# Graph network kernel, attention stage: scores computed with features on partitions, weights of batches and units drawn together, and a new order of the work on each engine

## The reference

```python
x = _layernorm(x + _L0_gnn_ref(x, L0_gnn_W, src, dst))      # three hops, then x @ W.T
edge_feat = concatenate([x[src], x[tgt]], axis=1)           # 256 values per edge
h = relu(edge_feat @ W1 + b1)                               # 128 values
w = sigmoid(h @ W2 + b2)[:, 0]                              # one weight per edge
agg = segment_sum(w[:, None] * x[src], tgt, num_segments=3125)
out = _layernorm(_layernorm(x + agg) * gamma + beta)        # outer norm of the residual sum left out here
```

## Time and profile before

| | before |
|---|---|
| median of 3 runs | 1422.31 us (1417.19 to 1425.18) |
| profiled execution: its own time | 1416.73 us |
| its span, first to last instruction | 1415.0 us |
| mean granted clock of TensorE | 0.831 |
| busy: PE, DVE, ACT, POOL | 1016.7 (72%), 980.4 (69%), 672.6 (48%), 655.3 (46%) us |
| gathers (L891) | 464, from 573.5 to 1346.3 us |
| moved by the gathers' queue | 60.85 MB |

### The profile page before, as it was taken

How to read it: one execution, slowest core, us unless ns; L and a number is a source line. 1 busy time by engine, 2 the same in 40 slices (tenths; PEclk the granted TensorE clock), 3 DMA queues, 4 the chain that set the end, 5 groups by cost and what they waited for, 6 DMA issues and landing times.

```text
span 1415.0 us, 32758 instructions
## 1 busy us (share of the span) xinstructions
PE 1016.7 (72%) x9885; PEld 784.0 (55%) x9886; DVE 980.4 (69%) x3477; ACT 672.6 (48%) x2508; POOL 655.3 (46%) x789
## 2 busy tenths in 40 slices
PE   4766665998998999236776777667686776777870
PEld 3656565777787877124554555445455554555550
DVE  7988887899998886136566656555565665566677
ACT  6555555211000222026655666556565656566676
POOL 1000001366743676755555565545556565555602
PEclk9999999999999999558678768667768787877785
DMA  2000000000000111535454455445445554544511
GB/s 82 1 0 0 0 0 1 1 3 3 2 3 4 38 41 52 142 116 144 133 148 140 141 150 147 122 121 144 140 135 157 143 145 127 153 138 144 153 34 47
DMA packets 77263, 120.07 MB, mean 85 GB/s; under 512 B 20488, under 2 KB 39484, under 8 KB 77116
## 3 DMA queue, kind: packets, MB, share of 16 engines
q0 software_dynamic: 22272, 60.85, 15.5%
q1 hardware_dynamic: 54844, 57.44, 13.9%
HBM read 111.41 MB, written 6.81 MB: 84 GB/s over the span
## 4 chain that ended last, share of the span: by engine, by line
DVE 37%; PE 28%; another core or an unknown queue 14%; issue 12%; ACT 5%; POOL 2%; DVEq 1%; DMA 0%; ACTq 0%; POOLq 0%; SPq 0%
PE bank L1748 6%; DVE t L1346 5%; DVE stage L997 4%; DVE region L1412 4%; PE bank L1633 4%; PE bank L1835 3%; DVE region L1396 3%; DVE region L1428 2%; PE bank L1787 2%; ACT PQ L2104 2%; PE bank L1635 2%; PE bank L1848 2%; PE bank L1709 2%; DVE stage L1160 2%
## 5 line engine op out<-in xcount | busy, mean ns | idle before, releaser
L891 POOL DMA_INDIRECT region<-src_split,region x464 | 444.9, 959 | 328.2 <-PE bank L1802 113.0
L1346 DVE SCALAR_TENSOR_TENSOR t<-bank,vec 128x128 f32<-128x128 f32 x464 | 107.0, 286 | 198.0 <-remote 166.8
L1748 PE MATMUL bank<-U,region 128*128 128x256 f16 (+1 forms) x1875 | 235.2, 276 | 3.8 <-DVE U L1137 2.1
L1826 PE MATMUL bank<-xs,region 128*128 128x128 f16 x572 | 130.8, 250 | 131.5 <-DVE region L1412 81.8
L2104 ACT ACTIVATE PQ<-region 128x128 f32<-128x128 f32 x572 | 169.7, 300 | 65.4 <-issue 37.4
L1748 PEld LDWEIGHTS bank<-U,region 128*128 128x128 fp8e4 x1875 | 178.8, 98 | 35.7 <-DVE U L1137 2.8
L2093 ACT CAST region<-bank 128x512 f16<-128x512 f32 x286 | 152.7, 579 | 89.6 <-remote 53.3
L1988 ACT CAST region<-bank 128x500 f32 x202 | 119.7, 593 | 92.2 <-PE bank L1635 68.4
L1826 PEld LDWEIGHTS bank<-xs,region 128*128 128x128 f16 x572 | 64.3, 112 | 150.5 <-issue 150.2
L1828 PE MATMUL bank<-region 128*128 128x128 f16 x572 | 134.7, 256 | 13.0 <-issue 12.9
L1848 PE MATMUL bank<-region 128*128 128x256 f16 x572 | 124.4, 349 | 24.9 <-issue 20.7
(11 more groups left out here) (272 smaller groups left out, 2360.2 us busy)
## 6 DMA issues: line engine op xcount, KB each, us to landing
region<-slot_rows SPq DMA_DIRECT2D x143, 256.0 KB
region<-src_split,region POOLq DMA_INDIRECT x464
region<-in_dst_dram SPq DMA_DIRECT2D x116, 64.0 KB
region<-tgt_split SPq DMA_DIRECT2D x116, 16.0 KB
src_split<-U SPq DMA_DIRECT2D x25, 64.0 KB, 1.5
src_split<-xs SPq DMA_DIRECT2D x25, 64.0 KB, 1.5
tgt_split<-q SPq DMA_DIRECT2D x25, 64.0 KB, 1.6
slot_rows<-aggT SPq DMA_DIRECT2D x88, 3.2 KB
```

Of the source, the lines that this page charges most:

```text
L891: nc.gpsimd.indirect_dma_start(out=G[:, p * TPS + i, :], out_offset=None, in_=src_split, in_offset=bass.IndirectOffsetOnAxis(ap=listed[n % ...
L1346: z = nc.vector.scalar_tensor_tensor(out=spare[i][:, :], in0=bank[q % 2][:, i * P:(i + 1) * P], scalar=0.0, in1=vec[:, W2, :], op0=ALU.max ...
L1748: z = nc.tensor.matmul(bank[2 * (k % 2) + p][:, 0:width], count[:, h, b * P:(b + 1) * P], U[k % 2][:, h, 0:width], start=h == 0, stop=h == ...
L1826: nc.tensor.matmul(to, here, p_table[:, h, 0:D], start=True, stop=False)
```

## The change

The score is no longer summed by DVE and ACT, but by PE. Before the hops, DVE takes the sign of W2 into a column `signs` and multiplies W1 and b1 by |W2|, so that the score becomes the sum over features of relu(...) * sign. In the loop:

1. PE computes P + Q with *features* on partitions and edges along the row (the operands of the products change places; L1810 and L1815 for a batch, L1875 and L1878 for a unit).
2. ACT takes relu of the whole 128x512 bank into float16 (`batch_relu`, `pair_relu`), and DVE the difference between the float32 relu and it (`batch_rest`, `pair_rest`), one instruction each.
3. PE sums both over the partitions by products with `signs`, one output column per tile: 8 products for a batch, 8 for a unit (`add_features`, for step s - 1), into bank 6.
4. One pair of sigmoids on ACT and one split on DVE serve batch and unit of a step together.
5. Order: `fetch_pair` stands ahead of `scored` in PE's step and `sums` at its end; `sums` and `sum_pair` follow their batch or unit by three steps and not by two. ACT and DVE take the unit first, DVE begins with `add_sums` and ends with the split and the weighing. SP loads a unit's slots one step earlier.
6. Buffers: `turned_hot`, `hot_weights` and `ohW` get three, `y_rows` four. `STEPS` is 149, and the batches are spread over the first 146.

The core of the diff (left out: buffers, semaphores, the checks of input ranges, the new places of folding):

```diff
+            link(nc.vector.tensor_tensor(yT[:, :], vec[:, W2, :], x3T[:, :], ALU.mult))
+            nc.vector.tensor_tensor(w1s[:, :, :], w1s[:, :, :],
+                                    yT[:, :].unsqueeze(1).broadcast_to([P, 2, D]), ALU.mult)
...
-                for i in range(m):
-                    z = nc.vector.scalar_tensor_tensor(
-                        out=spare[i][:, :], in0=bank[q % 2][:, i * P:(i + 1) * P], scalar=0.0, in1=vec[:, W2, :],
-                        op0=ALU.max, op1=ALU.mult, accum_out=zs[q % 2][:, i:i + 1])
+            def batch_rest(b):
+                dve.wait_ge(batch_high, b + 1)
+                nc.vector.scalar_tensor_tensor(
+                    out=relu_low[BATCH][b % 2][:, :], in0=bank[b % 2][:, :], scalar=0.0, in1=relu_high[BATCH][b % 2][:, :],
+                    op0=ALU.max, op1=ALU.subtract).then_inc(batch_low, 1)
...
+            def pair_rest(u):
+                dve.wait_ge(pair_high, u + 1)
...
-                    for half in range(2):
-                        z = nc.tensor.matmul(bank[q % 2][:, i * P:(i + 1) * P],
-                                             ohT[p][q * QR:(q + 1) * QR, i * P:(i + 1) * P],
-                                             qwin[p][q * QR:(q + 1) * QR, half * D:(half + 1) * D],
+                        z = nc.tensor.matmul(bank[q % 2][:, i * P:(i + 1) * P],
+                                             G[:, first + i, half * D:(half + 1) * D], ident16[:, :],
                                              start=False, stop=i == m - 1 and half == 1)
                 z.then_inc(s_psum, 1)
...
+            def add_features(s):
+                b, u = batch_at[s], unit_at(s)
...
+                if b is not None:
+                    pe.wait_ge(batch_low, b + 1)
+                if u is not None:
+                    pe.wait_ge(pair_low, u + 1)
+                if scored_steps(s) > 1:
+                    pe.wait_ge(w_ready, scored_steps(s) - 1)
...
+                    for i in range(TPB):
+                        to = bank[6][:, kind * TPB + i:kind * TPB + i + 1]
+                        nc.tensor.matmul(to, relu_high[kind][k % 2][:, i * P:(i + 1) * P], signs[:, :],
+                                         start=True, stop=False)
+                        z = nc.tensor.matmul(to, relu_low[kind][k % 2][:, i * P:(i + 1) * P], signs[:, :],
+                                             start=False, stop=True)
+                z.then_inc(z_psum, 1)
...
                 if u:
-                    pe.wait_ge(pair_z_ready, u)
+                    pe.wait_ge(pair_low, u)
...
+                if 0 <= u < TOTAL:
+                    fetch_pair(u)
                 if b is not None:
                     scored(b // BPS, b // BPS % 2, b % BPS)
-                    if b >= 2:
-                        sums((b - 2) // BPS, (b - 2) // BPS % 2, (b - 2) % BPS)
-                if 0 <= u < TOTAL:
-                    fetch_pair(u)
-                if 0 <= u - 2 < TOTAL:
-                    sum_pair(u - 2)
+                if s:
+                    add_features(s - 1)
+                if 0 <= u - 3 < TOTAL:
+                    if u == 3:
+                        pe.wait_ge(flag_ready, 1)
+                    sum_pair(u - 3)
...
+                if b is not None and b >= 3:
+                    sums((b - 3) // BPS, (b - 3) // BPS % 2, (b - 3) % BPS, blocks_folded(s - 1))
...
+                if 0 <= u < TOTAL:
+                    pair_relu(u)
+                    copy_rows(u)
                 if b is not None:
-                    sigmoids(b // BPS, b // BPS % 2, b % BPS)
+                    batch_relu(b)
+                if s and (batch_at[s - 1] is not None or unit_at(s - 1) is not None):
+                    sigmoids(s - 1)
```

More of the change, by code:

```diff
@@ L69, in gnn_kernel, with unit_at, scored_steps, batches_until @@
     for b in range(BATCHES_POOLED):
-        batch_at[b * STEPS // BATCHES_POOLED] = b
+        batch_at[b * (STEPS - 3) // BATCHES_POOLED] = b
+    def unit_at(s):
+        return s - LEAD if 0 <= s - LEAD < TOTAL else None
+    def scored_steps(s):
+        return sum(batch_at[k] is not None or unit_at(k) is not None for k in range(s + 1))
+    def batches_until(s):
+        return sum(b is not None for b in batch_at[0:max(s + 1, 0)])
+    def units_until(s):
+        return min(max(s + 1 - LEAD, 0), TOTAL)
+    FOLD_STEP = UNITS + 4 + LEAD
+    def batches_summed(s):
+        return max(batches_until(s) - 3, 0) if s < STEPS else BATCHES_POOLED
+    def blocks_folded(s):
+        return sum(due(k, FOLD_STEP, UNITS, DENSE - 1) is not None for k in range(s + 1))
+    def columns_at(s):
+        return 0 if batch_at[s] is not None else TPB, TPB if unit_at(s) is None else 2 * TPB
     def due(at, first, every, end):
@@ L298, in gnn_kernel @@
         Qs = [PQ[i][:, D:2 * D] for i in range(2)]
+        relu_high[BATCH] = [PQ[i][:, :].bitcast(f16) for i in range(2)]
         q16 = [sb(f"q16{i}", [P, 2, D], f16) for i in range(2)]
@@ L301, in gnn_kernel @@
         tiles_before = sb("tiles_before", [P, 1], f32)
-        spare = t1 + t2
-        unused = [PQ[i // 2][:, i % 2 * D:(i % 2 + 1) * D] for i in range(4)]
         ident16 = sb("ident16", [P, P], f16)
@@ L306, in gnn_kernel @@
         ws = [sb(f"ws{i}", [P, TPB], f32) for i in range(2)]
-        wsplit = [sb(f"wsplit{i}", [P, TPB, 2], f16) for i in range(2)]
-        ohW = [sb(f"ohW{i}", [P, TPB, 2, JW], f16) for i in range(2)]
+        ohW = [sb(f"ohW{i}", [P, TPB // 2, 2, 2, JW], f16) for i in range(3)]
         fbn = [[sb(f"fbn{r}{i}", [P, GROUP, 6], f32) for i in range(2)] for r in range(2)]
@@ L1510, in _ @@
                 b = batch_at[s]
[L1511 to L1519 removed]
+                after = None if s == 0 or batch_at[s - 1] is None else batch_at[s - 1] + 1
+                if after is not None and after % BPS == 0:
+                    first = load_four(ET.DVE, base[4], after // BPS, N)
+                attend(s, b, after, None if first is None else first[(after or 0) % BPS])
+            last_firsts = [dve.value_load(base[4][0:1, b + 4:b + 5], min_val=0, max_val=N)
+                           for b in range(BATCHES_POOLED - 3, BATCHES_POOLED)]
+            for b, first_target in zip(range(BATCHES_POOLED - 3, BATCHES_POOLED), last_firsts):
                 add_sums(b, b % BPS, first_target)
@@ L1778, in scored @@
                     pe.wait_ge(ohT_ready, n + 1)
-                if not (is_static(b) and b < 2):
-                    pe.wait_ge(z_ready, b - 1)
+                if b >= 2:
+                    pe.wait_ge(batch_low, b - 1)
+                for half in range(2):
+                    nc.tensor.matmul(bank[q % 2][:, 0:m * P], qwin[p][q * QR:(q + 1) * QR, half * D:(half + 1) * D],
+                                     ohT[p][q * QR:(q + 1) * QR, 0:m * P], start=half == 0, stop=False)
                 pe.wait_ge(gathered[p * BPS + q], 32 * (n - p) + 16 * m)
-                for half in range(2):
-                    nc.tensor.matmul(bank[q % 2][:, 0:m * P].rearrange("p (t k) -> p t k", k=P), ident16[:, :],
-                                     G[:, first:first + m, half * D:(half + 1) * D], start=half == 0, stop=False)
                 for i in range(m):
@@ L1803, in sums @@
                                              G[:, tile, (2 + y_half) * D:(3 + y_half) * D],
-                                             ohW[q % 2][:, i, w_half, :], start=i == 0 and y_half + w_half == 0,
+                                             ohW[b % 3][:, i // 2, w_half, i % 2, :], start=i == 0 and y_half + w_half == 0,
                                              stop=i == m - 1 and y_half == 1)
```

286 lines of the change are left out of this document (143 added, 143 removed).

## The result

The changed kernel takes 1412.9 us (median of 17 runs, 1410.6 to 1415.7), the kernel before 1422.2 us (17 runs, 1417.1 to 1430.4): ratio 0.9943, 95% interval 0.9925 to 0.996. It is faster by 0.6%, where 3.6% slower was forecast. A second set gave 1414.1 against 1419.1 us, 0.996 (0.9939 to 0.9981). The two profiled executions, 1412.6 and 1415.0 us, are closer than the medians, so I read sizes from two profiles of each kernel.

The account below looks back on a forecast made before the run. The prediction took POOL's gather cycle, with PE's increments held, as the bound. Longer pauses (+48) and the start (+3) summed to +51 us, 1473 against the median 1422.3; range 1410 to 1530.

Parts of the forecast that it names:

- The bound: Gather stage: POOL's cycle bounds, as PE's semaphore increments are held until about 1.0 us after a batch's last gather.
- The step that failed: PE's step after a release: 18 of 46 products, `sums` included, exceed the run-ahead limit, lengthening POOL's pause by 0.9 us.
- the +48: POOL's pauses: half of 107 grow by 0.9 us because `sums` comes after the release, +48 us.
- The mean of the pauses: POOL's pause before a gather batch: 2.0 us on average, 0.57 above 1.43.
- DVE and ACT at 0: Both engines get lighter, but neither is the bound, so their relief was costed at 0.
- One-column products: PE's step: priced at the 0.026 us spacing of `sums` products, 0.42 us a step at full clock.
- Their 72 us: PE's added work over the stage from one-column products, taken as hidden in PE's 27% idle time if the order is right.
- The start: Before `sums` of batch 0: three more hand-overs, mostly within the long hold, then two links and half a PE step, +3 us.
- C: Rival, faster: deeper buffers and three-batch lag get `agg_psum` out before each release; pauses fall to 1.43 us: -61, 1361; chance 0.17.
- B: Rival: the run-ahead limit does not bind; only PE's longer step shows, in cycles at half clock: +18, 1440; chance 0.20.
- D: Rival, much slower: every pause grows by 1.4 us, from one-column weight loads or `add_features` needing its own release: +150, 1572; chance 0.15.

Follow-up runs that it names:

- columns_less: The changed kernel without the eight one-column products of the relu's lower parts: 1218.6 us, ratio 1.0051 to the kernel before, which takes 1212.7 there.

## Why the prediction was wrong

**The bound** was read rightly for the chip of the first runs: POOL's cycle, PE's increments held until about 1.0 us after the last gather; without gathers a step falls from 5.4 to 3.65 us.

**The step that failed** is "`agg_psum` is ready at R + 1.35 + 4.4 ... behind `pair_psum` ... stand 46 products, and 28 can be issued", and with it the +48. I let PE's step begin at the release with `fetch_pair`. It does not: at the release PE stands in the step before, with `scored` or the one-column products still to issue. These, `sum_pair` and `sums` need less of this release than `fetch_pair` does. In the cycle shown, with the release near 877.7, the one-column products need the sigmoid that ends at 878.23 and `sums` needs the `add_sums` that ends at 879.20, both there before PE comes to them; the relu and the difference for `fetch_pair` take until 879.80. So `sum_pair` starts at 879.06 and `sums` at 879.86, 4.1 us and more ahead of the release near 884.0 at which they come out, and both ahead of the 10 products of `fetch_pair`. The first increment held is that of the one-column products, with `sums` only 4 products behind it; what is left over for after the release is work that POOL does not wait for. `pair_psum` is held, as forecast, and `fetch_pair` waits for its relu and difference, as forecast, but `sums` no longer stands behind them. The mechanism itself exists: with 8 or 16 more products `sums` falls behind the release in 65 and 79 of 80 cycles. The cost of the 16 is near what it says, but not its pattern: `sums` is late in nearly all cycles, and the ordinary pauses grow by 0.34 us on average, where I had 0.9 in half of them.

**The mean of the pauses** was a mean over two kinds. "Half of 107 pauses grow by 0.9" had no such cause: the extra 0.57 us over 1.43 was the 25 long ones. I had the rows for it (148 steps, 116 batches) and did not sort them.

**DVE and ACT at 0** was wrong. In a long pause nothing hides the round: 0.69 us more of DVE cost 16.7 us in all, and the change took the long pauses from 3.57 to 2.86 us, 0.7 x 24 = 17 us. How much of that is the relief and how much the new order on the engines no run separates. I had written that it would matter "were PE's increments free", and in one cycle of four they are. The other pauses grew by 0.1, 7 us over the same batches.

**One-column products** at 0.026 us: 0.025 measured. The Trainium skill (TensorE: Matmul & The Clock Gate, LDWEIGHTS) gives 107 ns for the load of 128 columns. The load's row shows 96 ns each without gathers, near it, but their spacing shows that this is not what a product adds. Their 72 us were taken for hidden, and in the changed kernel that was not tested downwards; upwards the next eight are not hidden.

**The start** at +3: +3.2, and +4.5 in the second profiles; of it 2.3 and 2.1 us lie behind the first gather, the rest is its own start, which differs by 2.6 us between runs that are alike up to it. That the sum is met so closely is in part luck. So is that 1412.9 us lies in the range given: its lower end came from C.

**The rivals:** B (the limit does not bind) had the mechanism, but its +18 left out the gain in free rounds, and its "quarter" at half clock was misread: a mean of 0.75 is half of the time at 1.2 GHz; C had the sign, from buffers that would end all long pauses, which did not happen; D's price of a weight load fell.

**Still open:** what the run-ahead limit counts (in the cycle shown 26 products go out behind the first held increment, the last two after standing 0.36 us, but PE stood 3 products behind the one-column products with 16 more of them); and why gathers take 969 ns after the change and 958 before (953 with `sums` first).

## What to carry to other kernels

Where a loop pauses for a semaphore, sort its pauses by what each iteration holds before taking a mean; the extra iterations may be all of the loss. An engine with idle time still sets the length of a round in just those iterations in which nothing hides it. And to say what stands behind a held increment, follow one full cycle from where the engine really stands at the release, not from the top of its step.

## What the runs showed of the chip that was not expected

The holding of PE's increments is not a property of the kernel alone. On three of the chips the kernel before takes 1417 to 1421 us (1422 in the first runs), on two others 1213 us, 15% less, with no holding. One of the slightly altered kernels there (`columns_less`), POOL's group from 600 us on, and below it order of time (L1873/L1876 `fetch_pair`, L2142 the relu that waits for it):

```profile
L920 POOL DMA_INDIRECT region<-src_split,region x444 | 427.9, 964 | 135.3 <-issue 131.9 <-PE bank L1850 3.4
```

```profile
1001.63 0.96 POOL L920 DMA_INDIRECT region<-src_split,region  x1 [0.30 <-issue]
...
1002.53 0.38 PE L1876 MATMUL bank<-region 128*128 128x256 f16 x2
1002.90 0.98 POOL L920 DMA_INDIRECT region<-src_split,region  x1 [0.30 <-issue]
1002.95 0.60 ACT L2142 ACTIVATE region<-bank 128x512 f16<-128x512 f32 x1 [0.59 <-PE bank L1876]
1004.18 0.94 POOL L920 DMA_INDIRECT region<-src_split,region  x1 [0.30 <-issue]
```

The product ends at 1002.91 and ACT starts 0.04 us later, in the middle of POOL's gathers; on the other chips this takes until a microsecond after the last of them. A gather is as long (964 ns), and the pauses are the 0.30 us between any two: 135.3 us for 444, not 317.5. What differs between the chips no run showed. All four versions of the changed kernel that ran there were 0.5 to 0.8% slower than the kernel before, even the one with less work than it; the changed kernel itself did not, so that it would be slower there too is only argued.
